# A Mamba block with a mixture of experts: statistics of the first pair ahead of the gates, unused expert tiles between the experts, part of y on ScalarE, and a new order of all engines

## The chip, the cores and the metric

The kernel is one program on one core of a Trainium2 chip. A core has five engines that run side by side, each through its own queue and strictly in order: TensorE (PE, matrix products and transposes into PSUM), VectorE (DVE), ScalarE (ACT), GpSimd (POOL) and SyncE (SP, which here only issues transfers). They meet at semaphores: an instruction waits until a counter has reached a value, and whatever stands behind it in its engine's queue waits too. Sixteen DMA engines move the data; the transfers are issued by SyncE, and the indirect ones, whose rows are addressed by a list, by GpSimd. The metric is the time of one execution on the device in microseconds.

## The reference

The input x is 16 sequences of 512 tokens with 128 features. In short, and with the shapes that matter:

```python
sa, ca, ga, sb, cb, gb = silu(c) @ wmod          # per sequence; |ga|, |gb| at least 0.25
h  = layernorm(x) * (1 + ca) + sa
# state-space layer: 4 heads of 64, state of 128, convolution over 4 steps
z, xBC, dt = split(h @ W_in.T)                   # 256, 512, 4
x_, Bm, Cm = split(silu(causal_conv(xBC) + conv_b))
dt = softplus(dt + dt_bias); dA = exp(-dt * exp(A_log))
# over t: H = H * dA[t] + (dt*x_)[t] outer Bm[t];  y[t] = H @ Cm[t] + D * x_[t]
y  = rmsnorm(y * silu(z)) * norm_w
x  = x + ga * (y @ W_out.T)
# mixture of experts: 8 experts, the two best for each token
h  = layernorm(x) * (1 + cb) + sb
topv, topi = top_k(h @ Wg.T, 2); w = softmax(topv)
# expert e: (silu(h @ W1[e].T + b1[e]) * (h @ W2[e].T + b2[e])) @ W3[e].T + b3[e], inner width 256
x  = x + gb * (w[0] * expert[topi[0]](h) + w[1] * expert[topi[1]](h))
```

All of it is in float32, and the output is x, 8192 x 128.

## The kernel before, in words

**Pairs and chunks.** The 16 sequences are worked off as 8 pairs (p, or f where it is the pair in the first half of its way). A pair of 1024 tokens is 8 blocks of 128 rows. The recurrence runs in 4 chunks of 128 steps (c). Within a chunk it is a masked product (`decay` times `gm`, `mix_chunk`, then `intra` into the PSUM bank YA); between chunks a state is carried (`new_state`, `next_state`, and `inter` into bank YB). `y_chunk(p, c)` puts chunk c of y together: the state's part is YB weighted by `edge` (L928), the chunk's own part is YA (L932), then the skip term (L934) and the gate (L935). For chunk 0 there is no state. The bank S is shared by many short products, and bank T (two halves) by the projections, the transposes and the convolution, which reads its taps from it (`conv_taps`, L868, three operations each).

**Experts.** After the second normalisation each token's two experts are known (`top_two`, `which_two`, `ranks`, `rows`). GpSimd writes each token's normalised row, the gate and its weight twice into a buffer `rows` in HBM, sorted by expert (`scatter(p, q)`, q = 0 to 7, two indirect DMAs each, L426). The expert work goes by tiles of 256 rows of one expert. A tile is full only when enough tokens have come, so `new_tiles(p)` lists, after each pair, which tiles can be started. There are 71 tiles in the program, whatever the routing is: 64 would hold all 16384 rows if every expert's count were a multiple of 256, and 7 more are there for the remainders. Tiles that the routing leaves unused are worked off like the others, on a dump area with rows of their own. The last list is made after the last pair; it covers tiles 49 to 70 (`LAST` = 22 of them), and its unused tiles come last.

For a tile t, SyncE loads the expert's weights (`load_weights`, 386 KB) and the rows (`load_rows`, 258 KB); TensorE turns the rows (`expert_turn`, L1380), makes the two up-projections (`expert_up`, L1390) and the down-projection (`expert_down`, L1403); ScalarE copies the turned rows and takes the silu (L654, L647); VectorE multiplies (`expert_hidden`, L1077) and weights the output (`expert_out`, L1085); GpSimd adds the 256 rows to the output in HBM with two indirect DMAs that accumulate (`add_out`, L456). There are 4 buffers of weights and 7 of rows. Two tiles of different experts can hold the same token, so their adds must not be in flight together. `add_out(t)` therefore waits until tile t-2 has landed, and until tile t-1 has landed too for all tiles up to 49 and, behind them, wherever tile t is the first of its expert (a value in `turn_of`, from which GpSimd takes what to wait for). Tiles of one expert never share a token.

**Order.** The order of each engine's queue is written out by hand as one long loop body per engine, over an iteration number i. In iteration i of before, pair i is in its recurrence, pair i+1 in its convolution, pair i+2 in its first normalisation, pair i-1 in routing, and the tiles 8i-27 to 8i-14 pass through the engines. GpSimd also has the powers -0.5 (`power_norm1`, `power_y`, `power_norm2`, L378), the products for the decay (`masked_da`, L416) and the weightings of x (`weight_by_dt` L399, `weight_by_decay` L408). Rows of the last pair can be loaded only when its 16 scatters have landed (`scattered` in `load_rows`), and the scatters stand between adds in GpSimd's queue.

**Start.** VectorE waits for the constants, makes some copies of them, then the gate values from the product that TensorE makes, and only then takes the statistics of pair 0 (`moments1(0)`), whose power GpSimd takes, whose shift VectorE makes (`shift_norm1(0)`), and with which ScalarE normalises (`normalise1(0)`, L533).

## Time and profile before

| | |
|---|---|
| median of 3 runs | 878.79 us (876.68 to 880.53) |
| profiled execution | 880.45 us, span 878.7 us |
| busy: TensorE, VectorE, GpSimd, ScalarE | 698.0, 606.1, 544.6, 448.2 us |
| instructions of GpSimd | 398, of which 142 indirect adds and 128 indirect scatters |
| mean granted TensorE clock | 0.895 |

The span runs from the first to the last instruction on the core. It has three parts. Up to about 117 us the pipeline fills. From there to 642.6 us pair follows pair. Then there is no recurrence left: up to 740.9 us the last pair is routed and scattered, and from 740.9 us on the last tiles run. A table of busy times by stretches, such as the first group of rows below, shows which of these parts an engine fills. An engine's busy time leaves out what its queue spends on issuing, so GpSimd, which issues 270 indirect DMAs, is fuller than it looks.

### The profile page before, as it was taken

To read this page: it belongs to the slowest core of one execution; us is meant where nothing else is said; L and a number is where in the kernel's file an instruction comes from. 1 tells how busy PE (TensorE), PEld (TensorE's weight loads), DVE (VectorE), ACT (ScalarE), POOL (GpSimd) and SP (SyncE) were. 2 spreads that over 40 slices of the span, in tenths; PEclk is the share of its full clock that TensorE was granted. 3 is DMA by queue.
4 is the path that set the end of the run, shared out by engine and by line. 5 is a ranking of instruction groups with operands and counts; after the bars stand their busy time and mean duration, and the time that the engine had idled before them with its cause. 6 is when DMAs were issued, how large, how long until landed. Compare 5 with 4: busy or idle time off the path is not lost. (4 is left out here: it accounts for less than half of the span.)

```text
span 878.7 us, 13494 instructions
## 1 busy us (share of the span) xinstructions
PE 698.0 (79%) x3713; PEld 533.7 (61%) x3713; DVE 606.1 (69%) x1618; ACT 448.2 (51%) x967; POOL 544.6 (62%) x398
## 2 busy tenths in 40 slices
PE   1578888798698899979998998999957851966773
PEld 1347557567467677756876686768746641645552
DVE  2548969989987998999899979986654440312221
ACT  2564675675676677648666666466423210312120
POOL 1215315647647678877877787778686666355556
PEclk9889698699798999999999999899988885988787
DMA  6000001111114533752564146434736785657673
GB/s 182 8 1 1 0 25 37 49 49 61 49 55 128 148 82 92 180 121 60 131 175 120 32 115 163 120 78 100 199 81 154 195 206 119 149 111 156 132 152 32
DMA packets 81273, 88.85 MB, mean 101 GB/s; under 512 B 7360, under 2 KB 67696, under 8 KB 81200
## 3 DMA queue, kind: packets, MB, share of 16 engines
q1 hardware_dynamic: 54528, 61.37, 24.3%
q0 software_dynamic: 26672, 26.62, 16.9%
q8 instruction: 32, 0.52, 0.3%
q14 instruction: 41, 0.34, 0.1%
HBM read 54.50 MB, written 33.46 MB: 100 GB/s over the span
## 5 line engine op out<-in xcount | busy, mean ns | idle before, releaser
L456 POOL DMA_INDIRECT out<-xs x142 | 229.8, 1618 | 133.6 <-issue 57.8
L426 POOL DMA_INDIRECT rows<-payload,pos x128 | 134.4, 1050 | 47.1 <-issue 31.2
L868 DVE SCALAR_TENSOR_TENSOR xbc<-T,table,xbc 128x511 f32<-128x511 f32 (+2 forms) x192 | 141.7, 746 | 8.3 <-ACT xbc L605 3.7
L1085 DVE SCALAR_TENSOR_TENSOR xs<-FX,xs 128x128 f32<-128x128 f32 x142 | 43.0, 344 | 102.5 <-PE FX L1403 91.6
L647 ACT ACTIVATE sg<-FG,wt 128x256 f32<-128x256 f32 x142 | 59.4, 471 | 100.2 <-PE FG L1390 95.4
L1403 PE MATMUL FX<-wt,hid 128*128 128x128 f32 x568 | 90.4, 307 | 20.1 <-DVE hid L1077 19.6
L1390 PE MATMUL FG<-xt,wt 128*128 128x256 f32 x284 | 84.2, 424 | 15.9 <-DMA wt<-in_wt 15.3
L1077 DVE SCALAR_TENSOR_TENSOR hid<-FV,wt,sg 128x256 f32<-128x256 f32 x142 | 61.9, 477 | 48.1 <-ACT sg L647 30.0
L1403 PEld LDWEIGHTS FX<-wt,hid 128*128 128x128 f32 x568 | 76.0, 208 | 30.4 <-DVE hid L1077 22.4
L1390 PE MATMUL FV<-xt,wt 128*128 128x256 f32 x284 | 82.8, 419 | 10.6 <-DVE hid L1077 10.4
L654 ACT ACTIVATE xt<-FX 128x256 f32<-128x256 f32 x71 | 27.2, 384 | 123.7 <-PE FX L1380 110.9
L1233 PE MATMUL T<-h,win 128*128 128x512 f32 x128 | 74.6, 693 | 14.4 <-DVE xbc L868 9.5
L416 POOL TENSOR_TENSOR mda<-table,da 128x1024 f32<-128x1024 f32 x32 | 65.3, 2117 | 27.6 <-DVE da L861 27.5
L1390 PEld LDWEIGHTS FG<-xt,wt 128*128 128x128 f32 x284 | 58.2, 216 | 33.9 <-DMA wt<-in_wt 16.8
L399 POOL TENSOR_TENSOR xdt<-tok,dt 128x512 f32<-128x512 f32 x32 | 48.3, 1508 | 44.9 <-ACT tok L572 39.6
L1292 PEld LDWEIGHTS YA<-xdt,decay 128*128 128x128 f32 x512 | 68.4, 211 | 5.7 <-ACT zs L617 4.2
L1390 PEld LDWEIGHTS FV<-xt,wt 128*128 128x128 f32 x284 | 56.8, 214 | 23.0 <-issue 16.4
L1292 PE MATMUL YA<-xdt,decay 128*128 128x64 f32 x512 | 69.3, 294 | 1.4 <-ACT zs L617 1.1
L605 ACT ACTIVATE xbc<-T,table 128x512 f32<-128x512 f32 x64 | 49.6, 775 | 40.7 <-PE T L1233 37.2
L1380 PE MATMUL FX<-table,xs 128*128 128x128 f32 x142 | 31.0, 303 | 40.6 <-DMA xs<-rows 23.3
L533 ACT ACTIVATE xn<-x,shift,rstd 128x128 f32<-128x128 f32 x128 | 50.9, 484 | 19.1 <-DVE shift L832 11.9
L378 POOL TENSOR_TENSOR rstd<-var,table 128x8 f32<-128x8 f32 x16 | 30.8, 1923 | 44.8 <-DVE var L814 44.8
(184 smaller groups left out, 1397.7 us busy)
## 6 DMA issues: line engine op xcount, KB each, us to landing
wt<-in_wt SPq DMA_DIRECT2D x71, 386.0 KB
xs<-rows SPq DMA_DIRECT2D x71, 258.0 KB
x<-in_x SPq DMA_DIRECT2D x8, 512.0 KB, 3.8
out<-x SPq DMA_DIRECT2D x8, 512.0 KB
out<-xs POOLq DMA_INDIRECT x142
rows<-pad SPq DMA_DIRECT2D x8, 258.0 KB
rows<-payload,pos POOLq DMA_INDIRECT x128
gate_a<-gates SPq DMA_DIRECT2D x8, 128.0 KB
```

The costliest lines, as they stand in the source:

```text
L416: nc.gpsimd.tensor_tensor(out=mda[:, c, :, :], in0=upto[:, :].unsqueeze(1).to_broadcast([P, 2 * NH, P]), in1=wide(da[:, c * J:(c + 1) * J] ...
L426: pool.indirect_dma_start(d["rows"], bass.IndirectOffsetOnAxis(ap=pos[:, k, n:n + 1], axis=0), payload[:, n, :], None).then_inc(scattered, 16)
L456: pool.indirect_dma_start(d["out"], bass.IndirectOffsetOnAxis(ap=xs[:, t % XSR, c, PAY - 1:PAY].bitcast(U32), axis=0), xs[:, t % XSR, c, 0 ...
L533: last = nc.scalar.activation(dst[:, j, :], src[:, j, :], ACT.Identity, bias=shift[:, j:j + 1], scale=rstd[:, j:j + 1])
L605: nc.scalar.activation(xbc[:, t, k, :], T[:, k, :], ACT.Identity, bias=conv_b[:, t:t + 1], scale=conv_w[:, t * KC + KC - 1:t * KC + KC]).t ...
L647: last = nc.scalar.activation(sg[:, t % 2, f * TR:(f + 1) * TR], FG[:, f * TR:(f + 1) * TR], ACT.Silu, bias=wt[:, t % WR, B12 + f:B12 + f ...
L868: last = nc.vector.scalar_tensor_tensor(out=xbc[:, t, k, tap:L], in0=T[:, k, 0:L - tap], scalar=w, in1=xbc[:, t, k, tap:L], op0=ALU.mult, ...
L1077: last = nc.vector.scalar_tensor_tensor(out=hid[:, t % 2, f, :], in0=FV[:, f * TR:(f + 1) * TR], scalar=wt[:, t % WR, B12 + FT + f:B12 + F ...
L1233: nc.tensor.matmul(T[:, k, :], win[:, o:o + P], h[:, k * L:(k + 1) * L], start=True, stop=True).then_inc(in_psum, 1)
L1292: last = nc.tensor.matmul(YA[:, o:o + HD], decay[:, c, k, hh, :], xdt[:, c % 2, k, hh * HD:(hh + 1) * HD], start=True, stop=True)
L1390: last = nc.tensor.matmul((FG, FV)[v][:, f * TR:(f + 1) * TR], wt[:, t % WR, w:w + P], xt[:, t % 2, :], start=True, stop=True)
L1403: last = nc.tensor.matmul(FX[:, TR + c * D:TR + (c + 1) * D], hid[:, t % 2, f, c * P:(c + 1) * P], wt[:, t % WR, DOWN + f * D:DOWN + (f + ...
```

## The change

**Statistics first.** `moments1(0)` stands ahead of the constants, and `shift_norm1(0)` ahead of the gate values on VectorE. On ScalarE `normalise1(0)` stands ahead of the copies of the modulation.

**Unused tiles between the experts.** The last list moves the start of each expert's tiles back by the number of experts before it that have tiles, at most by the number of unused tiles (`spread_spares`). So an unused tile stands behind each of the first experts, as long as there are some, and a tile that follows an unused one waits only for tile t-2.

**The state's part on ScalarE.** The multiplication of YB by `edge` on VectorE (one operation of 512 columns, with a broadcast) is replaced by eight activations of 64 columns with a scale of one value per row (`state_part`). VectorE's y of chunk 0 uses `faded` in place of `ysum`.

**Another order.** The loop body of every engine is another one, over another range of i. `gate_b` is loaded behind the store of x in place of beside `gate_a`. In the new numbering pair i-4 is in its recurrence.

The core of the diff:

```diff
+            def state_part(p, c):
+                act.wait_ge(yb_psum, (C - 1) * p + c)
+                act.wait_ge(edge_ready, p + 1)
+                wait(act, y_ready, C * p + (c if c > 1 else 0))
+                for n in range(J):
+                    d_ = slice(n * HD, (n + 1) * HD)
+                    last = nc.scalar.activation(ysum[:, d_], YB[:, d_], ACT.Copy, scale=edge[:, 0, c * J + n:c * J + n + 1])
+                last.then_inc(yb_taken, 1)
...
             def y_chunk(p, c):
...
-                vec.wait_ge(yb_psum, (C - 1) * p + c)
-                vec.wait_ge(edge_ready, p + 1)
-                nc.vector.tensor_tensor(out=ysum[:, :].rearrange("p (h d) -> p h d", d=HD),
-                                        in0=YB[:, :].rearrange("p (h d) -> p h d", d=HD),
-                                        in1=wide(edge[:, 0, c * J:(c + 1) * J], HD), op=ALU.mult).then_inc(yb_taken, 1)
                 vec.wait_ge(yb_taken, (C - 1) * p + c)
                 nc.vector.tensor_tensor(out=ysum[:, :], in0=YA[:, :], in1=ysum[:, :], op=ALU.add).then_inc(ya_taken, 1)
...
+            def spread_spares():
+                nc.vector.tensor_scalar(spare[:, :], seq_from[:, E:E + 1], -1.0, float(NTILES), ALU.mult, ALU.add)
+                link(nc.vector.tensor_scalar(some[:, :], tiles_new[:, :], 0.5, None, ALU.is_ge))
+                link(nc.vector.tensor_tensor(out=seq_part[:, :, :], in0=part["lower"].rearrange("p (a b) -> p a b", a=E + 1),
+                                             in1=some[:, :].unsqueeze(1).to_broadcast([P, E + 1, E]), op=ALU.mult))
+                link(nc.vector.tensor_reduce(out=rank[:, :], in_=seq_part[:, :, :], axis=AX.X, op=ALU.add))
+                link(nc.vector.tensor_scalar(rank[:, :], rank[:, :], spare[:, :], None, ALU.min))
+                link(nc.vector.tensor_tensor(out=seq_from[:, 0:E], in0=seq_from[:, 0:E], in1=rank[:, 0:E], op=ALU.add))
+                link(nc.vector.tensor_tensor(out=seq_to[:, :], in0=seq_from[:, 0:E], in1=tiles_new[:, :], op=ALU.add))
...
-                    link(nc.vector.tensor_tensor(out=tile_sum[:, 0:n], in0=tile_sum[:, 0:n], in1=begun[:, 0:n, E], op=ALU.add))
-                    nc.vector.scalar_tensor_tensor(out=turn_of[:, :], in0=tile_sum[:, 0:n], scalar=-32.0, in1=part["turn"],
+                    link(nc.vector.tensor_tensor(out=tile_sum[:, 0:n], in0=real[:, 0:n], in1=tile_sum[:, 0:n], op=ALU.subtract))
+                    link(nc.vector.tensor_tensor(out=need[:, 1:n], in0=tile_sum[:, 1:n], in1=real[:, 0:n - 1], op=ALU.mult))
+                    nc.vector.scalar_tensor_tensor(out=turn_of[:, 1:n], in0=need[:, 1:n], scalar=32.0, in1=part["turn"][:, 1:n],
                                                    op0=ALU.mult, op1=ALU.add).then_inc(turns_ready, 1)
...
+            moments1(0)
+            constants()
+            shift_norm1(0)
+            gate_values()
             set_pad_rows()
...
-            for i in range(-2, 13):
-                if is_pair(i):
-                    mix_chunk(i, 3)
-                    next_state(i, 0)
-                    y_chunk(i, 0)
...
+            for i in range(2, 16):
+                if is_pair(i - 6):
+                    new_tiles(i - 6)
+                if is_pair(i - 5):
+                    residual(i - 5)
+                    moments2(i - 5)
...
```

Here `real` is 1 for a tile with rows of its own, and `need` is 1 where a tile is its expert's first and the tile ahead of it is a real one.

How it moves the instructions is shown at three places. A row is one instruction form, or several alike in a row (x2), with the line of its kernel.

VectorE at the very start, before:

```order
L788 CAST before_r<-table 128x128
L789 TENSOR_SCALAR ones_r<-table 128x128
L791 TENSOR_SCALAR woutn<-mda,table 128x128 x2
L793 TENSOR_SCALAR nega<-exp_a 128x32
L795 TENSOR_SCALAR zs<-FV 16x256
L797 SCALAR_TENSOR_TENSOR zs<-zs,FV 16x256
L800 TENSOR_SCALAR zs<-zs 16x256
L802 SCALAR_TENSOR_TENSOR zs<-zs 16x256
```

and now:

```order
L832 BN_STATS stats<-x 128x6 x8
L834 TENSOR_TENSOR mv<-stats 128x8
L835 TENSOR_TENSOR apart<-stats 128x8
L836 TENSOR_TENSOR within<-stats 128x8
L837 SCALAR_TENSOR_TENSOR apart<-apart 128x8
L838 TENSOR_SCALAR within<-within 128x8
L839 TENSOR_TENSOR var<-within,apart 128x8
L812 CAST before_r<-table 128x128
L813 TENSOR_SCALAR ones_r<-table 128x128
L815 TENSOR_SCALAR woutn<-mda,table 128x128 x2
L817 TENSOR_SCALAR nega<-exp_a 128x32
L851 SCALAR_TENSOR_TENSOR shift<-mv,rstd 128x8
```

The statistics of pair 0 stand first, and its shift (L851) ahead of the gates (`zs` here is the space the gate values are made in).

VectorE from y of chunk 1 to y of chunk 2 in a middle pair, before:

```order
L928 TENSOR_TENSOR ysum<-YB,edge 128x512
L932 TENSOR_TENSOR ysum<-YA,ysum 128x512
L934 TENSOR_TENSOR ysum<-ysum,xskip 128x512
L935 TENSOR_TENSOR y<-ysum,zs 128x512
L1085 SCALAR_TENSOR_TENSOR xs<-FX,xs 128x128 x2
L868 SCALAR_TENSOR_TENSOR xbc<-T,table,xbc 128x511
L868 SCALAR_TENSOR_TENSOR xbc<-T,table,xbc 128x510
L868 SCALAR_TENSOR_TENSOR xbc<-T,table,xbc 128x509
L1077 SCALAR_TENSOR_TENSOR hid<-FV,wt,sg 128x256 x2
```

and now:

```order
L952 TENSOR_TENSOR ysum<-YA,ysum 128x512
L954 TENSOR_TENSOR ysum<-ysum,xskip 128x512
L955 TENSOR_TENSOR y<-ysum,zs 128x512
L1127 SCALAR_TENSOR_TENSOR xs<-FX,xs 128x128 x2
L1119 SCALAR_TENSOR_TENSOR hid<-FV,wt,sg 128x256 x2
L893 SCALAR_TENSOR_TENSOR xbc<-T,table,xbc 128x511
L893 SCALAR_TENSOR_TENSOR xbc<-T,table,xbc 128x510
L893 SCALAR_TENSOR_TENSOR xbc<-T,table,xbc 128x509
L1127 SCALAR_TENSOR_TENSOR xs<-FX,xs 128x128 x2
```

The first operation is gone (ScalarE's L594 makes what it made), and the expert outputs (L1127, before L1085) stand closer together.

GpSimd behind the last pair's recurrence, from its power for y on, before:

```order
L378 TENSOR_TENSOR rstdy<-ms,table 128x8
L426 DMA rows<-payload,pos 148224x258 x2
L456 DMA out<-xs 8960x128 x2
L378 TENSOR_TENSOR rstd<-var,table 128x8
L426 DMA rows<-payload,pos 148224x258 x2
L456 DMA out<-xs 8960x128 x2
L426 DMA rows<-payload,pos 148224x258 x2
L456 DMA out<-xs 8960x128 x6
L426 DMA rows<-payload,pos 148224x258 x4
L456 DMA out<-xs 8960x128 x2
L426 DMA rows<-payload,pos 148224x258 x4
L456 DMA out<-xs 8960x128 x2
```

and now:

```order
L382 TENSOR_TENSOR rstdy<-ms,table 128x8
L430 DMA rows<-payload,pos 148224x258 x2
L460 DMA out<-xs 8960x128 x2
L430 DMA rows<-payload,pos 148224x258 x2
L382 TENSOR_TENSOR rstd<-var,table 128x8
L430 DMA rows<-payload,pos 148224x258 x2
L460 DMA out<-xs 8960x128 x8
L430 DMA rows<-payload,pos 148224x258 x4
L460 DMA out<-xs 8960x128 x2
L430 DMA rows<-payload,pos 148224x258 x2
L460 DMA out<-xs 8960x128 x2
```

The scatter group of four (x4) is the first of the last pair in both. The adds (L460, before L456) ahead of it are four tiles in a row now and three in a row before, and the power for norm 2 (the second L382) stands one scatter pair later.

## Rows read from the trace of the kernel before

**Rows 1.** Busy by stretch: PE, PEld, DVE, ACT, POOL, PEclk, DMA share, GB/s.

```profile
413.40:496.70 83.30, 76.16 (x447) 59.48 (x446) 77.33 (x197) 55.02 (x118) 65.18 (x47) 0.98 0.48 118
...
642.60:740.90 98.30, 55.79 (x296) 45.16 (x296) 37.63 (x159) 20.65 (x50) 69.69 (x55) 0.78 0.62 146
...
773.90:874.30 100.40, 67.31 (x305) 51.03 (x304) 24.20 (x66) 17.77 (x45) 62.06 (x40) 0.82 0.61 118
```

**Rows 2.** VectorE's instructions in order (start, us), and line L941 alone.

```profile
413.37 0.68 DVE L941 TENSOR_TENSOR wo<-woutn,gate_a 128x512 f32<-128x512 f32 x1
...
486.63 3.65 DVE L934 TENSOR_TENSOR ysum<-ysum,xskip 128x512 f32<-128x512 f32 x1
...
496.68 0.68 DVE L941 TENSOR_TENSOR wo<-woutn,gate_a 128x512 f32<-128x512 f32 x1
...
L941 DVE TENSOR_TENSOR wo<-woutn,gate_a x8: 678/681/684, 116.3 to 642.6; 128x512 f32<-128x512 f32 x8
```

**Rows 3.** GpSimd's instructions in order, same stretch.

```profile
413.47 2.06 POOL L456 DMA_INDIRECT out<-xs  x1 [3.30 <-DVE xs L1085]
...
459.10 1.58 POOL L456 DMA_INDIRECT out<-xs  x1 [3.26 <-DMA out<-xs]
...
487.24 2.49 POOL L416 TENSOR_TENSOR mda<-table,da 128x1024 f32<-128x1024 f32 x1
```

**Rows 4.** Single lines: count, ns min/median/max, first and last start; ScalarE's timeline.

```profile
L928 DVE TENSOR_TENSOR ysum<-YB,edge x24: 671/682/693, 92.8 to 638.5; 128x512 f32<-128x512 f32 x24
...
L934 DVE TENSOR_TENSOR ysum<-ysum,xskip x24: 691/692/3655, 94.2 to 640.0; 128x512 f32<-128x512 f32 x24
...
L1020 DVE TENSOR_TENSOR row_of<-hot,row x8: 291/1554/4898, 158.6 to 684.7; 128x128 f32<-128x128 f32 x8
...
L525 ACT ACTIVATE mod<-FG x2: 177/180/184, 12.0 to 12.1; 128x16 f32<-128x16 f32 x2
...
L579 ACT ACTIVATE xskip<-tok,table x128: 386/392/411, 67.6 to 633.2; 128x128 f32<-128x128 f32 x128
...
444.86 1.27 ACT L579 ACTIVATE xskip<-tok,table 128x128 f32<-128x128 f32 x4
```

**Rows 5.** The start, in order of time; and the page's issue of x.

```profile
8.98 0.17 DVE L793 TENSOR_SCALAR nega<-exp_a 128x32 f32<-128x32 f32 x1
...
14.97 1.65 DVE L807 BATCH_NORM_STATS2 stats<-x 128x6 f32<-128x128 f32 x8
...
17.63 1.68 POOL L378 TENSOR_TENSOR rstd<-var,table 128x8 f32<-128x8 f32 x1 [13.91 <-DVE var L814]
...
19.61 3.19 ACT L533 ACTIVATE xn<-x,shift,rstd 128x128 f32<-128x128 f32 x8 [7.15 <-DVE shift L826]
...
22.94 1.94 PE L1211 MATMUL T<-table,xn 128*128 128x128 f32 x8 [9.96 <-ACT xn L533]
...
x<-in_x SPq DMA_DIRECT2D x8, 512.0 KB, 3.8
```

**Rows 6.** GpSimd from the last recurrence on, and TensorE's first turn after.

```profile
661.29 2.27 POOL L378 TENSOR_TENSOR rstd<-var,table 128x8 f32<-128x8 f32 x1
...
692.33 1.00 POOL L426 DMA_INDIRECT rows<-payload,pos  x1 [0.31 <-issue]
...
734.52 0.99 POOL L426 DMA_INDIRECT rows<-payload,pos  x1 [0.30 <-issue]
...
740.89 0.69 PE L1380 MATMUL FX<-table,xs 128*128 128x128 f32 x2 [18.23 <-DMA xs<-rows]
```

**Rows 7.** GpSimd's adds in the tail, in order.

```profile
751.91 1.55 POOL L456 DMA_INDIRECT out<-xs  x1 [5.82 <-DMA out<-xs]
...
773.88 1.55 POOL L456 DMA_INDIRECT out<-xs  x1 [4.32 <-DMA out<-xs]
...
777.59 1.55 POOL L456 DMA_INDIRECT out<-xs  x1 [0.30 <-issue]
...
785.29 1.55 POOL L456 DMA_INDIRECT out<-xs  x1 [4.29 <-DMA out<-xs]
```

967 lines of the change are left out of this document (495 added, 472 removed).

## The prediction

> **What bounds the kernel now.** I read the page's slices first (head, plateau, tail), then the busy time of each engine in stretches. In one pair of sequences in the plateau, 83.3 us, VectorE is busy 77.3, TensorE 76.2 and GpSimd 65.2 us [rows 1]. GpSimd is fuller than that: between two of its indirect DMAs it always has 0.3 us of "issue", and a pair has 32 of them (16 scatters, 16 adds), so its queue is taken for 65.2 + 9.6 = 74.8 us. Three engines are thus nearly full, VectorE the most. The period is 83.3 us from one L941 to the next; the seven of them between the first and the last L941 take 526.3 us, so the ones at the start and the end, with few expert tiles or without the next pair's convolution, are shorter (4 full ones, 3 short) [rows 2]. Behind the last pair's L941 at 642.6 come 98 us that end in the first rows routed by the last pair, and a tail in which no engine but GpSimd's queue keeps an even step [rows 1, 6, 7].
>
> VectorE's 77.3 us hold stalls. L934 takes 0.69 us as a rule and 3.65 once in this pair, beside a GpSimd product at 487.24; L1020 takes 0.29 at least and 4.90 at most, in this pair too [rows 2 to 4]. With smaller ones I count about 11 us of them in this pair. GpSimd's real waits in a pair are above all 3.3 us for VectorE's L1085 and 3.3 us for an add to land [rows 3].
>
> **The head.** Now VectorE prepares constants (done about 9.15), then the gates, and starts the first statistics at 14.97; the power follows at 17.63, the normalised x at 19.61 (3.19 us), TensorE's turn at 22.94 [rows 5]. After the change the statistics (1.65 us plus some 0.8 of small steps) stand ahead of the constants. x is the first transfer issued; if it is there by about 5.5 us, as the median of 3.8 us from issue to landing says [rows 5], they hide before 8.3. The power still needs the constants: 9.2 + 1.7 = 10.9, shift 11.1, normalise 11.2 to 14.4. ScalarE then does the four modulation copies, which start at 12.0 now [rows 4] with nobody waiting for them, and take about 0.5 us: the turn starts near 15.0. Gain 22.9 - 15.0 = 7.9 us; I take 7.5. The gates were cover for nobody: their values exist at 14.6 now and at about the same time then. If x is late, the gain falls to about 5.
>
> **The state's part of y.** VectorE loses 24 operations of 0.682 us (L928) with some 0.03 us each around them, 2.15 us per pair. Their least and longest are 671 and 693 ns: they never stalled, so their going takes no stall away. ScalarE gets eight activations of 64 columns for each. No row has that form; the nearest below is 16 columns out of PSUM, 180 ns each and 0.1 from one start to the next, and above it 128 columns, four in 1.27 us at 392 ns, 0.29 from one to the next [rows 4]. Eight cost between 0.8 and 2.5 us; between them by columns, about 1.4, and 4.2 us per pair. ScalarE is busy 55 of 83 us [rows 1] and can carry that, but VectorE now waits for it. Between y of chunk 1 and of chunk 2 VectorE has five other pieces (two taps of 2.3, two outputs of 0.6, one hidden of 0.9, and one output more), over 7 us, while ScalarE has the new part right after y 1; between chunks 2 and 3 it has 6.1 us, and TensorE must first do project_z, a down-projection and the state's product, which I add up to 4.4 us plus 1.4 to 2. Hidden, with a margin of a few tenths of a microsecond only in the second place. If the cover is gone, each microsecond of it costs 24.
>
> The Trainium skill ("SBUF — State Buffer", Who interferes with whom) says that a VectorE operation with two SBUF inputs and a GpSimd operation that reads SBUF exclude each other, and the loser is blocked to the end. The rows agree: L928 reads PSUM and never stretches, L934 reads SBUF twice and does. By that rule the time won at L928 can be lost again at L934 and L1020, wherever the new order lets them meet the products for the decay; that is part of the rivals' range below, and it speaks against counting the 2.15 us in full.
>
> **The order in the plateau.** GpSimd's adds move: the one that now waits 3.3 us for L1085 right ahead of the power for y stands there behind an output that is long done. Against it, two pairs of adds now have only one small product (1.5 us) between them, and up to tile 49 each add waits for the one before to land, about 4.3 us after its issue (the idle time before 785.29, and 3.26 behind a product before 459.10) [rows 3, 7]. That is 2.5 + 2.5 + 0.8 us of waits against 1.4 + 2.8 now. Net gain on GpSimd about 1.7 us: 81 to 82 us of 83.3. VectorE: 77.3 - 2.15 + some 5 us of idle = 80 to 81. I take 81.3 for the four full periods, 2.0 less each, and 1.9 less in the three short ones, where VectorE is just as full: 8.0 + 5.7 = 13.7, say 14 us. ScalarE's and TensorE's new places are costed at nothing, under VectorE's full queue; each stall of 1 us in a pair would take 7 us back.
>
> **From the last scan to the last pair's rows.** The power for norm 2 runs at 661.29, the last pair's first scatter starts at 692.33, its last at 734.52, and tile 49, the first that needs them, is turned at 740.89 [rows 6]. Between the end of that power and the first of these scatters GpSimd has two scatter pairs and four adds today, three of them in a row, 28.8 us; after the change one scatter pair and four adds in a row. An add costs 3.7 us to issue, and one that touches the next also 3.6 to 4.3 us of landing, so 2.6 + 3.7 + 3 x 7.3 = 28.3 us: the same. From the first scatter to the end of the last there are 16 scatters of 1.3 us, a copy of 1.8 and 5 adds of 3.7 today, 4 after the change: 43.2 us measured, about 40 then. From there to the add of tile 51 it is 38.4 us now (735.5 to 773.88 [rows 6, 7]) with six adds in the span; with five of 7.3 us, each waiting for the one before, less the first's wait, about 32. Together some 9 us; 2.6 go back, since the power for norm 2 stands one scatter pair later. I take 7, bounds 0 and 12.
>
> **The tail.** By the reference's router on these inputs 67 tiles are real and 4 unused; tiles 51 to 66 are two for each expert, 67 to 70 unused. The trace shows it: 773.88 and 777.59 follow at 3.71 us, then 7.70 us to 785.29, as the second expert waits for the first to land [rows 7]; there are seven such gaps up to tile 65, of 2.9 to 4.8 us, and none behind it. With the unused tiles between the first five experts four of seven waits lie behind an unused tile's 3.71 us: of about 4.1 us some 0.5 is left. 4 x 3.6 = 14.4 us. But supply may not follow at 3.71: the DMA engines' share is 0.61 of 100.4 us for 20 tiles, 3.1 us for each [rows 1], and that leaves a sixth of the step free. Taking a third off for that: 10 us, bounds 2 and 15. The new small VectorE operations that place the tiles (about ten of 0.2 to 0.4 us) run while GpSimd scatters.
>
> **Sum.** The profiled execution took 880.45 us with a span of 878.7. 880.45 - 7.5 - 14 - 7 - 10 = 842; it lies 1.7 above the median of the runs shown, so 840.
>
> **Rivals.**
> A, only the ends gain. GpSimd's queue sets the period: its 74.8 us plus landings that grow with the traffic (5.8 us of idle before 751.91 [rows 7]) fill 83 us again, and stalls at L934 eat the rest. For it: three engines full at once. Against: 3.3 us of GpSimd's wait has its cause removed. Time 840 + 14 = 854.
> B, the plateau does better: a lucky meeting of VectorE and GpSimd saves half of the 11 us of stalls as well, down to GpSimd's 78 us. 4 x 3.3 more, 827.
> C, slower. State part of y exposed: ScalarE runs in order, and state_part stands behind normalise (3.2 us) and z_silu, which wait for others. If VectorE stands for all of the upper bound, 2.5 us at each of 24 chunks, that is 60 us: 840 + 60 = 900. It decides where it eats the whole gain of 38.5 us, from 1.6 us a chunk. Against it: ScalarE is idle a third of the plateau.
> D, unused tiles don't do what they are put there for: the tail is held by weights and rows, whose loads stand in SyncE's queue behind landed adds, so each wait saved returns as a wait for data. 840 + 10 = 850.
>
> The Trainium skill ("Perfetto Trace Analysis", the rule on per-instruction overhead) puts ScalarE's fixed cost out of PSUM at about 51 ns; as an estimate from that page, 64 columns at 1.2 GHz add 53, so eight take 0.8 us. That is at the low bound of mine, and by it C would be out.
>
> **Chances.** Forecast 0.59, A 0.15, D 0.08, B 0.07, C 0.08, and 0.03 for gains and losses that cancel to within 0.5%, 4.4 us, which is about what a measurement can't tell from no change. So the same 0.03. Faster 0.89, slower 0.08. The forecast's own range is 830 to 851; to hold 8 in 10 with A, B and D it is 822 to 866.
>
> **What would show it.** First turn near 15 us; L928's operation gone from VectorE and no "DVE <- ACT ysum" above 0.3 us on average; L941-like period 81 us; first scatter of the last pair to first add of an unused tile without the seven gaps, three left of about 4 us. Wrong would be: a period at 83 or more (A), waits of VectorE for L594 of several us (C), TensorE waiting more for wt or xs in the tail than now (D).

## The result and the profile after

The changed kernel took 896.81 us (median of 4 runs, 894.3 to 902.41) beside 879.58 us for the kernel before (4 runs): ratio 1.0194, 95% interval [1.0156, 1.0231]. It is slower by some 2%, where 840 us was forecast. The profiled execution has a span of 892.6 us beside 878.7. Runs more than 1.5% above the fastest of their kernel are left out of every ratio that has an interval.

One mark per pair, VectorE's single instruction on the mean square (`ms`, L948 before and L968 after), divides both traces. It starts, in us:

| pair | 0 | 1 | 2 | 3 | 4 | 5 | 6 | 7 | last scatter | span |
|---|---|---|---|---|---|---|---|---|---|---|
| before | 116.9 | 184.8 | 251.8 | 330.4 | 414.0 | 497.3 | 580.0 | 643.2 | 734.5 | 878.7 |
| after | 107.4 | 175.0 | 243.7 | 338.2 | 427.4 | 522.3 | 605.6 | 678.9 | 762.6 | 892.6 |

The head is 9.5 us shorter. The seven periods together are 571.5 us instead of 526.3: 45.2 longer, of which 16.0, 5.6 and 11.7 in the third to fifth and 10.1 in the last. From the last mark to the last scatter it is 7.6 less, from there to the end 14.2 less. Sum: -9.5 + 45.2 - 7.6 - 14.2 = +13.9.

The head, in the timelines of VectorE, ScalarE and TensorE (beside [rows 5]):

```profile
4.76 1.65 DVE L832 BATCH_NORM_STATS2 stats<-x 128x6 f32<-128x128 f32 x8 [4.76 <-DMA x<-in_x]
...
11.30 3.18 ACT L539 ACTIVATE xn<-x,shift,rstd 128x128 f32<-128x128 f32 x8 [1.08 <-DVE shift L851]
...
14.52 0.23 ACT L533 ACTIVATE mod<-FG 128x16 f32<-128x16 f32 x2
...
14.81 1.97 PE L1258 MATMUL T<-table,xn 128*128 128x128 f32 x8 [1.68 <-DVE zs L827]
```

x was there at 4.76, and TensorE's first turn starts at 14.81 instead of 22.94. The last row puts that wait down to the gates (L827), but the kernel asks TensorE only for the second of the four gate steps, done at 14.02, and for the modulation copies (L533), whose last ends at 14.75: it is these that let it go.

The busy time by stretch, in the columns of [rows 1], for the fourth to seventh period:

```profile
338.20:427.40 89.20, 82.64 (x449) 64.40 (x447) 72.11 (x194) 59.68 (x142) 63.05 (x48) 0.92 0.46 110
427.40:522.30 94.90, 80.50 (x448) 62.59 (x447) 72.12 (x193) 59.60 (x142) 63.92 (x48) 0.91 0.44 104
522.30:605.60 83.30, 77.56 (x444) 59.88 (x442) 71.79 (x179) 57.29 (x135) 62.02 (x47) 0.98 0.46 112
605.60:678.90 73.30, 64.89 (x387) 52.24 (x386) 46.46 (x137) 40.33 (x113) 53.39 (x43) 0.95 0.52 125
```

VectorE's busy time fell by 5.3 us a pair in the fourth and fifth period and by 1.8 in the sixth, beside the 2.15 forecast. Stalls are in these differences, and they moved as well as went: L1020 took 4.90 us in the period of [rows 1], and its successor L1060 takes 0.29 in each of the fourth to sixth; but `first_row` (L1053, before L1013), 0.16 us as a rule, now takes 4.1 there, and `faded` (L927) 1.7 on average where L902 took 0.68. In the third to fifth period VectorE is idle for 17 to 23 us. What it waited for, from 243.7 to 522.3 (sum, times, longest, us):

```profile
DVE stats L832 <- DMA x<-in_x: 18.2, 3, 9.2
DVE xs L1127 <- PE FX L1450: 8.1, 6, 1.7
```

The first of these waits does not occur in the plateau before. SyncE's queue shows where it comes from; first after, then before:

```profile
448.27 1.60 SPq L314 DMA_DIRECT2D xs<-rows  x2
450.70 0.35 SPq L294 DMA_DIRECT2D wt<-in_wt  x1
...
454.91 0.38 SPq L314 DMA_DIRECT2D xs<-rows  x1
455.39 0.42 SPq L268 DMA_DIRECT2D x<-in_x  x1
```
```profile
434.62 0.38 SPq L262 DMA_DIRECT2D x<-in_x  x1
435.82 0.35 SPq L288 DMA_DIRECT2D wt<-in_wt  x1
```

Before, the reload of x goes out at 434.62 and its reader on VectorE runs at 440.03. There the reload stands one iteration ahead of its reader. After, it stands in the iteration of its reader, and four row loads (the first row shows two), two weight loads and the gates stand ahead of it in SyncE's order; the first of these row loads waits 9.6 us for scattered rows. x is issued at 455.39, though its buffer had been free since 446.5 (the end of normalise2). What stands behind x's reader on VectorE, and who waits for that:

```profile
462.12 1.64 DVE L832 BATCH_NORM_STATS2 stats<-x 128x6 f32<-128x128 f32 x8 [9.24 <-DMA x<-in_x]
...
464.54 0.60 DVE L1127 SCALAR_TENSOR_TENSOR xs<-FX,xs 128x128 f32<-128x128 f32 x2
```
```profile
465.29 0.66 PE L1427 MATMUL FX<-table,xs 128*128 128x128 f32 x2 [8.46 <-DVE xs L1127]
```
```profile
465.93 1.58 POOL L460 DMA_INDIRECT out<-xs  x1 [10.74 <-DVE xs L1127]
```

One late transfer holds VectorE 9.2 us, TensorE 8.5 and GpSimd 10.7: the output L1127 of an expert tile, for which both wait, is queued behind the statistics, and needs nothing of x. Over the run GpSimd's waits for that output are 95.7 us in 18, before 26.6 in 8.

The last stretch, GpSimd's adds (to [rows 7]), and the waits of GpSimd from the last scatter to the last add, first after, then before:

```profile
780.38 1.56 POOL L460 DMA_INDIRECT out<-xs  x1 [6.04 <-DVE xs L1127]
...
786.44 1.56 POOL L460 DMA_INDIRECT out<-xs  x1 [2.64 <-DMA out<-xs]
...
794.16 1.56 POOL L460 DMA_INDIRECT out<-xs  x1 [4.30 <-DMA out<-xs]
...
802.24 1.56 POOL L460 DMA_INDIRECT out<-xs  x1 [0.93 <-DMA out<-xs]
...
871.14 1.56 POOL L460 DMA_INDIRECT out<-xs  x1 [6.30 <-DVE xs L1127]
```
```profile
POOL out L460 <- DMA out<-xs: 18.9, 9, 4.3
POOL out L460 <- DVE xs L1127: 16.6, 4, 6.3
```
```profile
POOL out L456 <- DMA out<-xs: 35.2, 11, 5.8
...
POOL out L456 <- DVE xs L1085: 8.5, 3, 4.4
```

### The profile page after: what moved, and what is told of

It reads as the page before. It is cut to its first block and busy times, and to the rows that moved or that the text cites. A ratio compares the mean times of both kernels' runs of the same rounds, so it can differ in the third digit from the quotient of the medians.

```text
span 892.6 us, 13675 instructions
## 1 busy us (share of the span) xinstructions
PE 711.0 (80%) x3713; PEld 539.9 (60%) x3713; DVE 591.6 (66%) x1607; ACT 486.0 (54%) x1159; POOL 535.8 (60%) x398
## 5 line engine op out<-in xcount | busy, mean ns | idle before, releaser
L460 POOL DMA_INDIRECT out<-xs x142 | 225.5, 1588 | 167.3 <-DVE xs L1127 95.7
L1127 DVE SCALAR_TENSOR_TENSOR xs<-FX,xs 128x128 f32<-128x128 f32 x142 | 43.1, 345 | 81.6 <-PE FX L1450 81.3
L1450 PE MATMUL FX<-wt,hid 128*128 128x128 f32 x568 | 85.1, 294 | 11.4 <-DVE hid L1119 11.4
L1437 PE MATMUL FV<-xt,wt 128*128 128x256 f32 x284 | 82.9, 419 | 4.2 <-DVE hid L1119 4.2
L1450 PEld LDWEIGHTS FX<-wt,hid 128*128 128x128 f32 x568 | 71.4, 197 | 20.9 <-DVE hid L1119 12.9
L1280 PE MATMUL T<-h,win 128*128 128x512 f32 x128 | 73.3, 688 | 8.3 <-DVE xbc L893 6.8
L1339 PE MATMUL YA<-xdt,decay 128*128 128x64 f32 x512 | 72.9, 304 | 1.6 <-ACT zs L632 0.8
L1339 PEld LDWEIGHTS YA<-xdt,decay 128*128 128x128 f32 x512 | 71.5, 221 | 3.4 <-ACT zs L632 1.7
L620 ACT ACTIVATE xbc<-T,table 128x512 f32<-128x512 f32 x64 | 49.7, 777 | 36.2 <-PE T L1280 35.5
L1437 PEld LDWEIGHTS FV<-xt,wt 128*128 128x128 f32 x284 | 55.1, 210 | 14.8 <-issue 8.4
L382 POOL TENSOR_TENSOR rstd<-var,table 128x8 f32<-128x8 f32 x16 | 29.6, 1850 | 55.5 <-DVE var L839 49.7
L1427 PEld LDWEIGHTS FX<-table,xs 128*128 128x128 f32 x142 | 16.5, 147 | 74.4 <-issue 42.7
```

The costliest lines, as they stand in the source:

```text
L460: pool.indirect_dma_start(d["out"], bass.IndirectOffsetOnAxis(ap=xs[:, t % XSR, c, PAY - 1:PAY].bitcast(U32), axis=0), xs[:, t % XSR, c, 0 ...
L620: nc.scalar.activation(xbc[:, t, k, :], T[:, k, :], ACT.Identity, bias=conv_b[:, t:t + 1], scale=conv_w[:, t * KC + KC - 1:t * KC + KC]).t ...
L1280: nc.tensor.matmul(T[:, k, :], win[:, o:o + P], h[:, k * L:(k + 1) * L], start=True, stop=True).then_inc(in_psum, 1)
L1339: last = nc.tensor.matmul(YA[:, o:o + HD], decay[:, c, k, hh, :], xdt[:, c % 2, k, hh * HD:(hh + 1) * HD], start=True, stop=True)
L1437: last = nc.tensor.matmul((FG, FV)[v][:, f * TR:(f + 1) * TR], wt[:, t % WR, w:w + P], xt[:, t % 2, :], start=True, stop=True)
L1450: last = nc.tensor.matmul(FX[:, TR + c * D:TR + (c + 1) * D], hid[:, t % 2, f, c * P:(c + 1) * P], wt[:, t % WR, DOWN + f * D:DOWN + (f + ...
```

## The experiments

Ratios are to the kernel before, run on the same chip beside each; the chips differ, so ratios are compared and not microseconds. "Full periods" are the three from the mark of pair 3 to that of pair 6, 249.6 us together in the trace of before, 267.4 after. Each is one trace of one execution. e3 and e4, which change nothing in these periods, show 249.4 and 250.9, so a difference of 1 us says nothing. And the traces come from several chips: e1 to e4 and e13 to e15 from one on which the kernel before takes 879 to 880 us, e16 to e18 from one with 881, e5 to e12 from one with 885 to 886. On this last one there is no trace of the kernel before, and e12, which changes nothing in these periods either, has 258.2.

**e1 and e9, x's reload early.** In SyncE's list of the changed kernel:

```
+                if is_pair(i - 2):
+                    reload_x(i - 2)
                 if is_tile(PT * i - 55):
                     load_rows(PT * i - 55)
...
-                if is_pair(i - 2):
-                    reload_x(i - 2)
```

> The changed kernel with one move: in SyncE's list the reload of x for the next pair stands ahead of the row load of tile PT*i-55 instead of behind three row loads, three weight loads and the gates. Theory 1 (x comes late behind SyncE's row loads, VectorE stands in moments1 and with it expert_out, TensorE and GpSimd): the waits of VectorE on x's reload (7.0, 1.9 and 9.2 us in three periods, 23.0 us in 4 waits over the run) go, and those periods fall from 94.6, 89.2 and 95.0 us to 83 to 86, so the time is 868 us (860 to 876). Rival 2 (the new order of TensorE and VectorE makes long chains at the experts, x's wait only stood in their place): the waits on x go, but the periods stay above 89 us and the time stays at 888 to 900 us. Rival 3 (the state's part on ScalarE): no difference, 890 to 900 us.

> The changed kernel with x's reload ahead of the row load of tile PT*i-55, the same as in e1, for an interval (the four runs of e1 lay between 861 and 880 us) and as the base of the next two. Theory 1: ratio to the kernel before 0.980 to 0.993. Rival 2 (the order): 1.00 or more.

e1: 870.61 us beside 878.97, 0.9905, from four runs that spread from 861.27 to 879.99; the two lowest (861.27 and 866.86) would give 0.983. That is too few for an interval. e9, the same kernel, 12 runs on another chip: 883.3 beside 885.08, 0.9983 [0.9948, 1.0018]. The waits on x in the plateau are gone; only the first load, at the start of the kernel, is waited for (4.8 us). x is issued at 432.45, and its reader at 438.97 waits for nothing:

```profile
432.45 0.38 SPq L268 DMA_DIRECT2D x<-in_x  x1
434.23 1.61 SPq L314 DMA_DIRECT2D xs<-rows  x2
```

The waits go as theory 1 said. In time, one move in one queue takes back 2.1% by e9, some 19 us, and 2.9% by e1's median; the changed kernel itself was not run on e9's chip, so this compares ratios of two chips. e9 lies above theory 1's range (0.980 to 0.993) and its interval reaches 1.00, where the rival begins: x explains this much and not the whole. And the two traces of this one kernel differ in the full periods, e1 first, e9 second:

```profile
331.00:413.20 82.20, 75.53 (x448) 58.64 (x447) 74.26 (x193) 59.59 (x142) 64.48 (x48) 1.00 0.50 120
413.20:495.60 82.40, 75.94 (x449) 58.94 (x447) 73.90 (x194) 59.40 (x142) 64.19 (x48) 1.00 0.49 120
```
```profile
328.90:417.60 88.70, 80.83 (x449) 63.32 (x447) 71.00 (x194) 59.58 (x142) 63.14 (x48) 0.94 0.46 111
417.60:506.20 88.60, 82.30 (x448) 63.49 (x447) 71.70 (x193) 59.89 (x142) 64.56 (x49) 0.92 0.47 114
```

Same instructions, VectorE's busy time even less in e9: what is longer is TensorE's, 82.3 instead of 75.9, at a granted clock of 0.92 instead of 1.00, and the period is longer by as much. GpSimd's waits for expert outputs in the three full periods are 39.3 us in 9 in e9, 9.0 in 5 in e1, 13.3 in 4 in the kernel before. Long periods like these are not special to the new order: e12 (below), with the order of before, has on e9's chip

```profile
327.30:415.40 88.10, 81.64 (x457) 65.40 (x455) 76.65 (x196) 56.25 (x120) 64.79 (x48) 0.90 0.46 112
```

and 85.70 us at 0.92 in the next. e9's traced execution (891.49) is also one of the two slowest of its twelve.

**e6, x's reload late in the kernel before.** The opposite edit, all other orders as before:

```
                 if is_tile(PT * i - 20):
                     load_rows(PT * i - 20)
+                if is_pair(i + 2):
+                    reload_x(i + 2)
...
-                if is_pair(i + 3):
-                    reload_x(i + 3)
```

> The kernel before with x's reload put where the change puts it relative to the rows: for the same pair it stands an iteration later in SyncE's list, behind two row loads, all else as before. Theory 1: VectorE now waits for x in the full periods, 2 to 9 us each, and the queue behind its reader (expert_out, TensorE, GpSimd) waits with it: 10 to 25 us slower, 889 to 904 us. Rival (the kernel before has room for it, what the changed kernel lost needs its new order as well): below 883 us.

927.73 beside 885.91, 1.045 [1.0379, 1.0521]: 40 us, more than the 10 to 25 expected. The wait is larger here:

```profile
DVE stats L807 <- DMA x<-in_x: 48.0, 3, 17.1
```

The place of this transfer in SyncE's order is enough by itself to make the kernel slower.

**e5, the reader of x later.** moments1(i - 2) on VectorE moved behind expert_out(PT * i - 56) and conv_taps 0 and 1; SyncE as changed.

> The changed kernel with moments1 of the next pair (VectorE's reader of x) behind expert_out of tile PT*i-56 and the first two groups of convolution taps, about 12 us later in VectorE's list; SyncE's list as changed. Theory 1 (x late, and expert_out queued behind its reader): x is there by the time it is asked for, and expert_out no longer stands behind it, so the time is near that of the early reload, 866 to 876 us. Rival 2 (the new order elsewhere; the early reload gained by moving SyncE's row and weight loads relative to each other): 888 us or more.

901.15 beside 885.91, 1.0156 [1.0094, 1.0219]. Theory 1 expected near e1, 866 to 876 us; it failed here, and the number is the rival's (888 or more), though the waits on x in the plateau are gone. Another wait took their place, GpSimd before its power for norm 1, which needs these statistics and stands ahead of its adds:

```profile
POOL rstd L382 <- DVE var L839: 88.5, 10, 20.7
```

It was 49.7 us in 7 in the changed kernel. A late reader can cost as much as late data when an in-order queue elsewhere waits for what it makes. So this run decides nothing on SyncE's order; e1, e9 and e6, which move only the transfer, do.

**e2 and e10, the state's part of y on VectorE again**, in the changed kernel and in e9's (the three calls of state_part on ScalarE go):

```
-                    state_part(i - 4, 1)
...
             def y_chunk(p, c):
...
+                vec.wait_ge(yb_psum, (C - 1) * p + c)
+                vec.wait_ge(edge_ready, p + 1)
+                nc.vector.tensor_tensor(out=ysum[:, :].rearrange("p (h d) -> p h d", d=HD),
+                                        in0=YB[:, :].rearrange("p (h d) -> p h d", d=HD),
+                                        in1=wide(edge[:, 0, c * J:(c + 1) * J], HD), op=ALU.mult).then_inc(yb_taken, 1)
```

> The changed kernel with the state's part of y weighted on VectorE again, in one instruction just ahead of its reader (24 instructions of about 0.7 us back on VectorE, 192 short ones off ScalarE), all else as changed. Theory 1 (x late behind SyncE's rows, then the order): the part on ScalarE is worth little either way; VectorE is idle 17 to 23 us in a period, so the 2 us a period come partly out of idle time: 897 to 905 us. Rival 3 (the eight short activations a chunk hold back y and ScalarE's other work): the time falls by more than 8 us, below 889 us. The count of my forecast (each of the 24 worth its 0.68 us on VectorE) gives 897 + 14 = 911 us.

> The changed kernel with x's reload early and the state's part back on VectorE. With x late, the part on VectorE cost 18 us; there TensorE stood before the next chunk's state part (YB) until VectorE had read the last, 29.4 us in 8 waits. If the part is worth VectorE's time alone (24 pieces of 0.68 us and full periods on VectorE), this is 13 to 18 us above the run with x early: ratio 1.00 to 1.01. If what e2 lost came only from x late and the part together: within 5 us of it, ratio below 0.995.

e2: 914.68 beside 878.97, 1.041 [1.0331, 1.0488], which is 2.1% above the changed kernel's. e10: 898.86 beside 885.08, 1.0147 [1.0075, 1.0219], 1.6% above e9. The part on ScalarE brings 14 to 19 us in the new order; rival 3 is out. Theory 1's own number for e2 (897 to 905) failed: the count of the forecast, 911, is nearer. 24 pieces of 0.68 us are 16.4.

```profile
PE YB L1341 <- DVE ysum L940: 29.4, 8, 4.9
```

That wait in e2 is TensorE before the next state product, until VectorE has read the last out of PSUM; in e10 it is 26.0 us in 8, in the changed kernel and in e9 it does not occur. So with the part on ScalarE this bank is free in time. How much of the 14 to 19 us is this wait and how much is VectorE's own time, no run separates.

**e7, the state's part alone, in the order before.**

> The kernel before with only the state's part of y on ScalarE (eight short activations a chunk, in its list behind weight_by_d(2), expert_input(PT*i-20) and expert_input(PT*i-19)), all other orders as before. If VectorE's full list sets the period, as I forecast, the 24 pieces of 0.68 us come off it: 13 to 16 us faster, 863 to 866 us. If the period hangs as much on the chains between engines, as the changed kernel with the early reload suggests (its full periods are 82.2 to 82.4 us where VectorE is busy 74), only some 1 us a period comes: 870 to 876 us. If the eight activations stand in front of squares and expert inputs that are waited for: slower than before, above 881 us.

888.82 beside 885.91, 1.003 [0.9994, 1.0067]. Nothing, where 13 to 16 us were expected by the forecast's premise. VectorE had 73.2 us to do in the period from 416.0 instead of 77.3, and the period was 84.1 us. But over the run VectorE waited 10.6 us in 7 for ScalarE's ysum, a wait that the new order has once (2.1 us): rival C's mechanism, in the order of before. And TensorE's wait for VectorE before the next state product, 14.2 us in 3 in the kernel before, comes back as one of 11.1 us in 3 ahead of YA. So e7 does not take 16.4 us off VectorE and change nothing else; it shows that the edit is worth nothing in this order, not that VectorE has slack.

**e3 and e4, the head alone and the unused tiles alone, in the order before**, and **e12, both.**

> The kernel before with only the first pair's statistics (VectorE) and normalise1 (ScalarE) ahead of the constants and gates; orders, state's part and unused tiles as before. As in the changed kernel the first mean square moves from 116.9 to about 109 us and all later work follows: 7 to 9 us faster, 871 to 873 us. Rival: the later pairs take it back, because their rows and weights come at times set elsewhere: 878 to 880 us.

> The kernel before with only the unused tiles put between the experts in the last placement; all orders as before. Theory 1: of the seven waits of 4 us between the last output scatters some four go, 8 to 12 us off the end, 867 to 872 us, and nothing changes ahead of the last scatter of rows. Rival (the tail is held by the weights and rows that come one tile after another, the turn order only follows them; what was saved in the changed kernel came from its other order of the last pair): 0 to 3 us, 876 to 880 us.

> The kernel before with the first pair's statistics first and the unused tiles between the experts; order and state's part as before. Alone they gave 6.7 and 9.7 us; added, 16 us, ratio 0.981 to 0.983. The kernel that has the state's part on ScalarE too stands at 0.981: if this one is at 0.98 as well, the state's part is worth nothing in the order of before (as alone, 1.003); if it is above 0.988, the two edits overlap and the state's part does bring some of the 0.981.

e3: 872.32 beside 878.97, 0.9933 [0.9902, 0.9963]. e4: 869.29 beside 878.97, 0.9869 [0.9797, 0.9942]; from the last scatter to the end it takes 134.2 us instead of 144.2, and the last scatter starts at 736.6 instead of 734.5. Behind the first adds of that stretch, GpSimd's seven waits of 2.9 to 4.8 us (28.6 us together, from the add at 785.29 on) have become nine, 19.0 us together, six of them of 1.1 to 2.0 us. e12: 869.22 beside 885.08, 0.9799 [0.9737, 0.9862]: they add. It is faster than both kernels.

**e8, these two and the state's part, in the order before.**

> The kernel before with three of the four parts of the change (first pair's statistics first, unused tiles between the experts, state's part on ScalarE) and the order of before. Head alone gave -7, spares alone -10. If they add and the state's part brings its 14 us: 848 us; if the state's part brings 1 us a period only: 856 us (850 to 860). Theory 1 with 2 beside it (the new order costs beyond x's reload): faster than the changed kernel with the early reload (870 us) by 10 us or more. Rival (new order is neutral once x is early): 868 to 872 us.

869.25 beside 885.91, 0.9812 [0.9746, 0.9879]: the same as e12, so the state's part adds nothing here either (VectorE waited 14.8 us in 9 for ScalarE's ysum). Against e9 (0.9983), which has the same three parts and the new order with x early, on the same chip, the new order costs 1.7%. Of the 18.9 us between the two traces, 8.7 are in the six periods from the first mark to that of pair 6 (only 3.1 of them in the full ones, which are 88.8, 87.6 and 83.6 us long in e8), 6.0 from there to the last scatter and 6.2 behind it; the head is 2.0 shorter.

**e11, e9 without the spread of the unused tiles.**

> The changed kernel with x's reload early and the unused tiles at the end again. In the order of before the unused tiles between the experts were worth 9.7 us. If their worth does not hang on the order: 8 to 12 us above the run with x early, ratio 0.995 to 1.005, with the waits of some 4 us between the last output scatters back. If the new order's last pair already keeps GpSimd free of them: within 4 us of it.

877.4 beside 885.08, 0.9922 [0.9886, 0.9957]: 0.6% faster than e9, not slower as expected; the two intervals just touch. In the new order the edit brings nothing and may cost. In e9, GpSimd's waits from the last scatter to the last add are mostly for expert outputs and less for landings:

```profile
POOL out L460 <- DVE xs L1127: 33.9, 8, 10.3
...
POOL out L460 <- DMA out<-xs: 9.8, 6, 2.6
```

In e11 they are 17.5 us in 5 and 17.7 in 6, and the stretch from the last scatter to the end is 130.3 us where e9 has 137.6 and the changed kernel 130.0. But e9's traced execution lies 8 us above the median of its runs, and e1's trace of the same kernel has 127.6 us (landings 12.6 in 7, outputs 20.1 in 5), so these traces don't rank the two; the run times do, by 0.6%.

**e13 to e17, what sets the full periods of the kernel before.** e13 issues the last multiply of y_chunk 1 to 3 twice (VectorE); e14 every second matmul of project_in twice (TensorE); e16 masked_da(f, 0) twice (GpSimd). e15 leaves out the experts' bias matmul, and with it the bias; e17 lets masked_da 2 and 3 write m heads instead of 8:

```
e13 +                link(nc.vector.tensor_tensor(out=yc, in0=ysum[:, :]..., in1=gate, op=ALU.mult))
e14 +                if k == 0:
    +                    nc.tensor.matmul(T[:, k, :], win[:, o:o + P], h[:, k * L:(k + 1) * L], start=True, stop=True)
e15 -                nc.tensor.matmul(FX[:, TR:TR + 2 * D], sel..., b3_parts..., start=True, stop=False)
e16 +                if c == 0:
    +                    nc.gpsimd.tensor_tensor(out=mda[:, c, :, :], ...).then_inc(pool_step, 1)
    +                    pool.wait_ge(pool_step, f + 1)
e17 +                m = 2 * NH if f == 0 or c < 2 else 1
```

> The kernel before with the last multiply of each y_chunk 1 to 3 on VectorE issued twice (24 more of 0.69 us, 2.1 us a pair, same result). My forecast took VectorE's full queue for what sets the period of the middle; then the time is 14 to 17 us above before, ratio 1.016 to 1.019. If TensorE sets it and VectorE has slack (the state's part taken off VectorE alone brought nothing): ratio 1.000 to 1.005.

> The kernel before with every second matmul of project_in issued twice (4 more a pair of 128x512, 0.53 us each by the rows of the period 414.0 to 497.3, 2.1 us a pair, same result). If TensorE sets the period (76.2 us busy of 83.3 at a granted clock of 0.98): 14 to 17 us above before, ratio 1.016 to 1.019. If VectorE's queue sets it, as forecast: ratio 1.000 to 1.005.

> The kernel before without the matmul that adds the expert's output bias (71 of 0.28 us, 2.2 us a full period; the bias is left out of the result). If TensorE sets the period of the middle: 10 to 20 us faster, ratio 0.977 to 0.989. If VectorE's queue sets it: within 4 us of before in the middle, and at most 3 us at the end.

> The kernel before with masked_da(f, 0) on GpSimd issued twice (one more instruction a pair, 2.35 us by the rows of the period 414.0 to 497.3, same result). Theory 4 (GpSimd's queue, with the waits on VectorE's xs that come from its own additions one round earlier, sets the full periods; the 4.4 us a pair more on TensorE and 2.1 us more on VectorE moved none of them by over 1.4 us in four of the five full periods): the full periods grow by 1.5 to 2.4 us each and the time by 10 to 18 us, ratio 1.011 to 1.020. Rival (nothing but the chains between the engines sets it): the full periods stay at 83 to 84 us and the ratio below 1.006.

> The kernel before with masked_da(f, 2) and masked_da(f, 3) on GpSimd cut to one head of eight from the second pair on (some 4 us less on GpSimd a pair; the masks of half the chunks stay those of the first pair). Theory 4: full periods 79.5 to 81.5 us instead of 83.3, and 12 to 25 us less in all, ratio 0.972 to 0.987. Rival (TensorE with 76 us busy of 83, and VectorE with 77, take over at once): full periods above 82 us, ratio 0.990 or more.

| run | issued more or less, us a pair | that engine's busy time in the full periods together | full periods together | ratio |
|---|---|---|---|---|
| before | | | 249.6 | 1 |
| e13 | VectorE +2.1 | -1.2 | 253.8 | 1.0114 [1.0062, 1.0167] |
| e14 | TensorE +4.4 | +8.5 | 251.0 | 1.0213 [1.0143, 1.0284] |
| e15 | TensorE -2.3 | -7.0 | 238.6 | 0.9822 [0.9732, 0.9912] |
| e16 | GpSimd +2.35 (by the row) | +5.0 | 252.3 | 1.0065 [1.0038, 1.0092] |
| e17 | GpSimd -3.4 | -10.2 | 243.1 | 0.9915 [0.9883, 0.9947] |
| e7 | VectorE -2.15 | -11.2 | 253.1 | 1.003 [0.9994, 1.0067] |

The two columns in the middle differ because an engine's busy time holds stalls and overlaps, and these give way: e13 issues 6 us more on VectorE, and VectorE is not busier. e7 is from the chip without a trace of before, so only its ratio compares.

My count for e14 was wrong by half: a product of 512 columns is two instructions, so 64 were added and not 32. By the profile the line went from 74.6 us to two of 41.2 and 68.8. One of its full periods, with the same length as before:

```profile
430.95:514.34 83.39, 78.67 (x452) 62.13 (x452) 74.25 (x196) 54.19 (x118) 65.12 (x48) 0.96 0.48 118
```

GpSimd's waits in that period are, to 0.1 us, those of before, above all 6.7 us for expert outputs and 3.3 for a landing. So none of the three sets the full periods alone. 8.5 to 13 us of TensorE's work on the three periods cost 1.4, which a second trace could undo; 6 of VectorE's cost 4.2 (3.5 of them in one, at a clock of 0.90 instead of 0.96), 5 to 7 of GpSimd's 2.7. Taking 10 us off GpSimd gives 6.5 back, and taking a matmul out of each expert tile's own chain (e15) 11.0 for 7. Over the whole run, e13 costs 10.0 us for 16.6 issued, e14 18.7 for 35.4, e16 5.7 for 13.1 of busy time, and e17 gives 7.5 for 22.5: 0.3 to 0.6 of the amount each. e14's and e13's cost lies mostly in the first periods and the head, where there is less to hide it. Theory 4, GpSimd alone, expected 10 to 18 and 12 to 25 us and is out. The forecast's premise, VectorE alone, expected 14 to 17 for e13; the upper end of e13's interval, 14.7, just reaches that, so it is unlikely and not excluded by this run alone. e14 speaks against it more clearly: by it TensorE's extra work, of which the expectation counted half, would have cost under 5 us.

**e18, e9 with e17's cut of masked_da.**

> The changed kernel with x's reload early and the same cut of masked_da. If GpSimd sets the full periods in the new order too, they fall by 2 to 4 us each and the ratio is 12 to 25 us below that of the reload alone (0.998): 0.970 to 0.985. If in the new order the chain TensorE, VectorE, GpSimd at the experts sets them (GpSimd waited 99 us for VectorE's xs there, 27 us in the kernel before): ratio 0.990 or more.

864.35 beside 880.55, 0.9799 [0.977, 0.9828], 1.8% below e9. Its full periods are 83.0, 83.0 and 82.9 us at clock 1.00, 1.00 and 0.98: no shorter than e1's (82.2, 82.4, 81.8), 2.9 to 5.7 shorter than e9's. The ratio is within the range expected if GpSimd set the periods, but the three traces come from three chips, so it stays open whether the cut of masked_da or the clock, 0.98 to 1.00 here as in e1 and 0.92 to 0.96 in e9, makes this difference.

```profile
410.41:493.44 83.03, 76.02 (x448) 58.80 (x447) 73.58 (x194) 59.51 (x142) 61.58 (x47) 1.00 0.48 119
```

## Why the prediction was wrong

- **The head** was right, in its path too: 7.5 us forecast, TensorE's first turn 8.1 us earlier and let go by the modulation copies, 6.7 us alone in e3.
- **The state's part** had its size right: eight activations take 1.75 us (bounds 0.8 to 2.5, 1.4 taken), VectorE waited for them once, 2.1 us, and rival C (900 us, nearest in its number) did not occur in the changed kernel; that its number lies near is chance. Its wait did occur in the order of before (e7). The row:

```profile
471.47 1.75 ACT L594 ACTIVATE ysum<-YB,edge 128x64 f32<-128x64 f32 x8
```

  By the Trainium skill ("Perfetto Trace Analysis", Optimizing Scalar/DVE Operations) the prediction estimated 0.8 us for the eight; the trace does not agree, and the measurement decides.
- **The order in the plateau** is the step that failed, and with it the sign. It said: "ScalarE's and TensorE's new places are costed at nothing, under VectorE's full queue". SyncE's new order it did not cost at all, although the change puts the reload of x into the iteration of its reader, behind four row loads. Shown: x late makes waits of 9.2, 7.0 and 1.9 us on VectorE, taking it back gives 2.1% (e9), and making it late in the order before costs 4.5% (e6). The gain that the step did count, 1.7 us a pair on GpSimd, did not come either: in the full periods GpSimd's waits for expert outputs, to be removed, went from 13.3 us in 4 to 41.0 in 9. With x early they are 9.0 in one trace (e1, full periods 1.1 us shorter each where 2.0 was forecast) and 39.3 in the other (e9). The forecast also counted four full periods; there are three, and the one ahead of them is 78.6 us long.
- **The premise under it**, that VectorE's queue sets the period so that each microsecond off it is a microsecond off the pair, is not borne out: added work costs 0.6 of itself on VectorE (e13) and 0.5 on TensorE (e14), and moving the state's part gives nothing in the order of before (e7, e8), where VectorE then waits for ScalarE. In the new order that part is worth its 14 us (e2, e10), and there TensorE's wait for a PSUM bank goes with it. Rival A ("only the ends gain") describes the order of before: e12 and e8, 0.980 and 0.981, gain what the ends give alone (6.7 and 9.7 us). It named GpSimd's queue as the cause, which e16 and e17 bear out by less than half.
- **From the last scan to the last pair's rows**, -7 forecast and -7.6 measured is no hit. The period ahead of that mark grew by 10.1 and holds more expert work (43 GpSimd instructions in it instead of 38; e8, with the order of before, has 43 and 71.5 us there too). From the mark of pair 6 to the last scatter it is 157.0 us instead of 154.5.
- **The tail**: -10 forecast for the unused tiles. Alone, in the order before, they give 9.7 us (e4), by the mechanism forecast: shorter waits for landings where unused tiles stand between (1.1 to 2.0 us, 0.5 forecast). In the new order the end is 14.2 us shorter, but not through them: e11 has as short an end without them. Landings cost less there with the edit (9.8 and 12.6 us in e9 and e1, 17.7 in e11), outputs more (33.9 and 20.1, 17.5 in e11). That is rival D's outcome and not its cause: TensorE's waits for rows and weights in the tail are 21.4 us in the changed kernel and 36.7 in the kernel before.
- **What is left of 1.0194.** Late x is 2.1% of it. The new order's remaining 1.7% against e8 is located and not explained: 6.0 us between the mark of pair 6 and the last scatter, 6.2 behind it, and 2 to 3 in each of the second, third and sixth period; the full periods of some 88 us are in e8 and e12 too and are no part of it. What sets 83.3 us is not settled either. The probes leave the ring add, landing, row load, TensorE, VectorE, add as the candidate. Only e15 shortens it, and e15 shortens TensorE's queue as well: it fits, and shows nothing by itself.

## What to carry to other kernels

When a change rewrites the order of all engines, go through the DMA-issuing queue first: for each load ask when its buffer is free, what now stands ahead of it that waits, and what its reader holds up. That three engines are 78 to 93% busy does not say which of them sets the pace; adding two microseconds to each, one at a time, tells more, and here it found that none did alone. Such a probe needs more than one trace: here two traces of the same stretch differed by 1 us on one chip and by 9 between two. Measure the parts in the old order before taking the new one: two parts here were worth 2.0% without it. But a part can also be worth more in the new order than in the old, as the state's part was.

## What the runs showed of the hardware

- One kernel ran its full periods in 82.2 us at a granted clock of 1.00 and in 88.6 us at 0.92 to 0.94, with the same instructions, on two chips (e1, e9). The clock's upper level is 2.4 GHz, and 1.00 is that level throughout. TensorE's busy time was 75.9 and 82.3 us, as much apart as the periods. Not every product is longer: the 128x512 products of L1280 take 707 ns on average at 0.92 and 595 at 1.00, the 128x128 ones of L1450 288 in both.
- In the changed kernel's fourth and fifth period, with waits for x of 1.9 and 9.2 us on VectorE, the granted clock is 0.92 and 0.91; in the kernel before, without such waits, 0.98 [rows 1]. The three periods with late x are 33.3 us longer than before; 5.9 of that is still there in e1's third period, and of the other 27.4 the waits for x are 18.2. That the clock makes the rest fits the rows; it was not tried, and e12 shows 0.90 and 0.92 without any late x.
- Eight activations of 64 columns out of PSUM take 1.75 us, 0.2 from one start to the next. Four of 128 columns out of SBUF, as many columns in all, take 1.27 [rows 4].
